# Moving work at the seams of a two-layer image kernel: moments of x, dummy matmuls, two normalisations and the last taps

## The reference

```python
# layer 0: linear attention, 6 heads of 64
x = x + attn(_gn(x))     # q, k = elu(rope(W x + b)) + 1 ; v = W x + b
                         # kv = sum_n k v ; out = q kv / (q . sum k + 1e-6) ; 1x1 conv Wfc
# layer 1: gated convolution
t = 1x1 conv(_gn(x))     # w_in
t = irfft2(rfft2(t, 8x8 patches) * fft_filter)
t = depthwise 3x3 conv(t); x1, x2 = halves of t
x = x + 1x1 conv(gelu(x1) * x2)   # w_out
# _gn: 32 groups of 12 channels, mean and variance over the group and all pixels
```

## Time and profile before

| | |
|---|---|
| median of 3 runs | 3602.86 us |
| the profiled execution's own time | 3610.5 us |
| its span, first to last instruction | 3608.4 us |
| PE busy | 3351.8 us (93%) |
| DVE busy | 3006.7 us (83%) |
| POOL busy | 2046.6 us (57%) |
| ACT busy | 1709.3 us (47%) |
| mean granted TensorE clock | 0.976 |

### The profile page before, as it was taken

The page is one execution under the profiler, slowest core; times in us unless marked ns, Lnnn a source line. Parts: engine busy times, 40 slices in busy tenths (PEclk is TensorE's granted clock), DMA queues, the critical chain, the costliest instruction groups (busy, mean ns, idle before and its releaser), DMA issues. The chain is left out here.

```text
span 3608.4 us, 50305 instructions
## 1 busy us (share of the span) xinstructions
PE 3351.8 (93%) x17430; PEld 2901.3 (80%) x17430; DVE 3006.7 (83%) x5252; ACT 1709.3 (47%) x3138; POOL 2046.6 (57%) x1343
## 2 busy tenths in 40 slices
PE   5999989999899999999999999999999999999998
PEld 4987779777797777977789777897778967799776
DVE  7977988779897698987989869788798887988877
ACT  1433844338443474434744357342574426644265
POOL 2554755547556474564755647456474565654555
PEclk9999999999999999999999999999999999999999
DMA  6214332143312333123321233312332133321422
GB/s 220 71 45 158 115 105 72 61 149 108 119 63 67 135 120 108 62 79 123 132 97 62 97 115 124 104 62 100 120 123 97 53 123 105 123 90 60 140 97 96
DMA packets 185339, 369.89 MB, mean 103 GB/s; under 512 B 7770, under 2 KB 8834, under 8 KB 184834
## 3 DMA queue, kind: packets, MB, share of 16 engines
q1 hardware_dynamic: 185090, 366.68, 29.7%
HBM read 265.99 MB, written 100.66 MB: 102 GB/s over the span
## 5 line engine op out<-in xcount | busy, mean ns | idle before, releaser
L1124 PE MATMUL bank<-w_hi,x_hi 128*128 128x384 f32 x2304 | 803.1, 349 | 19.3 <-ACT vt L575 10.0
L444 POOL TENSOR_TENSOR t<-t 128x768 f32<-128x768 f32 x256 | 534.8, 2089 | 468.8 <-DVE t L829 464.8
L1125 PE MATMUL bank<-w_lo,x_hi 128*128 128x384 f32 x2304 | 778.8, 338 | 0.0
L993 DVE SCALAR_TENSOR_TENSOR bank<-big,wdw,bank 128x512 f32<-128x512 f32 x1072 | 750.5, 747 | 22.4 <-PE bank L1305 19.4
L437 POOL TENSOR_TENSOR x_lo<-xa,x_hi 128x512 fp32r<-128x512 f32 x360 | 459.0, 1290 | 526.0 <-ACT x_hi L564 526.0
L509 POOL TENSOR_TENSOR prod<-prod 128x512 f32<-128x512 f32 x320 | 412.2, 1288 | 256.5 <-ACT prod L667 238.1
L1129 PE MATMUL bank<-w_hi,x_lo 128*128 128x384 f32 x2304 | 531.5, 339 | 0.5 <-POOL x_lo L437 0.5
L569 ACT ACTIVATE t<-t 128x384 f32<-128x384 f32 x256 | 134.7, 526 | 767.5 <-POOL t L444 749.9
L1124 PEld LDWEIGHTS bank<-w_hi,x_hi 128*128 128x128 f32 x2304 | 434.1, 188 | 26.4 <-issue 25.8
L1125 PEld LDWEIGHTS bank<-w_lo,x_hi 128*128 128x128 f32 x2304 | 434.9, 189 | 2.3 <-issue 1.7
L1129 PEld LDWEIGHTS bank<-w_hi,x_lo 128*128 128x128 f32 x2304 | 413.4, 188 | 1.4 <-POOL x_lo L437 1.4
(11 more groups left out here) (131 smaller groups left out, 7042.9 us busy)
## 6 DMA issues: line engine op xcount, KB each, us to landing
xr<-x SPq DMA_DIRECT2D x128, 768.0 KB, 4.8
xa<-x SPq DMA_DIRECT2D x64, 768.0 KB, 6.3
x_scratch<-xr SPq DMA_DIRECT2D x64, 768.0 KB, 3.3
xa<-x_scratch SPq DMA_DIRECT2D x64, 768.0 KB, 6.0
xr<-x_scratch SPq DMA_DIRECT2D x64, 768.0 KB, 4.9
out<-xr SPq DMA_DIRECT2D x64, 768.0 KB, 3.3
big<-x SPq DMA_DIRECT2D x8, 768.0 KB, 10.2
w_raw<-wqkv_t SPq DMA_DIRECT2D x1, 1728.0 KB, 7.0
```

Source lines behind the costliest of these rows:

```text
L444: nc.gpsimd.tensor_tensor(a, a, b[:, :, ::-1, :], ALU.add).then_inc(s_add, 1)
L993: nc.vector.scalar_tensor_tensor(dst, src, wdw[:, k, q:q + 1], so_far, ALU.mult, ALU.add)\
L1124: nc.tensor.matmul(dst, hi(k), whi(k), start=(k == 0), stop=False)
L1125: nc.tensor.matmul(dst, hi(k), wlo(k), start=False, stop=False)
```

## The change

Five edits, all of order or place. No arithmetic changes except that the next image's first chunk is normalised by ACT in the form x * rstd + shift instead of by DVE in the form (x - mean) * rstd.

1. The three `bn_aggr` of x leave `group_norm` and become `x_moments`, which DVE runs at the head of step 7 of stage B.
2. Dummies between the two averages: 2 instead of 6. After the second: 7 instead of 10.
3. In step 1 of stage C, ACT normalises and rounds chunk 2 right after its second `copy_t`, and POOL's `low_part` of it stands after two of the five additions.
4. In step 7 the next image's first chunk is normalised by ACT, at the place where steps 2 to 6 have their `normalise`.
5. In step 8 PE runs both sets of taps before the out blocks of chunk 6; in step 9 DVE runs all taps and both gates first, then the residuals of chunk 6, then `rope` of the next image. PE's wait ahead of `project` is split by block.

```diff
@@ part_c, gpsimd
+                    if c == 1:
+                        for k in range(KB):
+                            low_part(i * 16 + c + (NCH + 1), k, 1 - par, patches=(edge != NCH - 1))
...
-                    if within(edge, 0, NCH if i + 1 < images else NCH - 1):
+                    if c != 1 and c < (NCH if i + 1 < images else NCH - 1):
@@ part_c, scalar
                     if tile:
                         copy_t(T + 1, 1)
+                    if c == 1:
+                        normalise(1, i * 8 + 5 + h + par, 1 - par)
+                        high_part(i * 16 + c + (NCH + 1), 1 - par, patches=True)
...
-                        if within(edge, 0, NCH, 1) and edge != 0:
-                            normalise(i * 8 + 5 + h + par, 1 - par)
+                        if 1 < c < NCH - 1:
+                            normalise(1, i * 8 + 5 + h + par, 1 - par)
                         copy_img(T + 1, c, 1)
...
                         if edge == NCH - 1 and i + 1 < images:
+                            normalise(0, i * 8 + 9, 0)
                             high_part(i * 16 + 16, 0)
@@ vector
+            def x_moments(f):
+                dve.wait_ge(s_stat, f * NCH + NCH)
+                for k in range(KB):
+                    nc.vector.bn_aggr(mv[:, 0, k], bn_x[:, k].rearrange("p c s -> p (c s)"))
...
                 def part_b(c, h, edge, par):
+                    if c == NCH - 1:
+                        x_moments(i + 1)
...
                     if last:
-                        for m, early in enumerate((LAST[0:2], LAST[2:4], LAST[4:6])):
-                            for q, k in early:
-                                tap(c - 2, q, k, last)
-                            add_out(3, m)
+                        for q, k in LAST[:6]:
+                            tap(c - 2, q, k, last)
                         gate_narrow(c - 2, last)
-                        if i + 1 < images:
-                            rope((i + 1) * NT, 0, 0)
                         for q, k in LAST[6:]:
                             tap(c - 2, q, k, last)
                         gate_wide(c - 2, last)
+                        for m in range(KB):
+                            add_out(3, m)
+                        if i + 1 < images:
+                            rope((i + 1) * NT, 0, 0)
                         for m in range(KB):
                             add_out(2, m)
...
-                    if edge == NCH - 1 and i + 1 < images:
-                        normalise(0, i * 8 + 9, 0)
@@ tensor
                 keep_warm(14, 0)
-                group_avg(i + 1, 6, 0)
-                keep_warm(10, 0)
+                group_avg(i + 1, 2, 0)
+                keep_warm(7, 0)
...
                         taps(c - 1, 0, PE_LAST[0])
+                        taps(c - 1, 1, PE_LAST[1])
                         for b in range(KB):
                             out_block(c - 2, b)
-                        taps(c - 1, 1, PE_LAST[1])
                     if last:
-                        pe.wait_ge(s_res, (i * 16 + c + NCH - 2) * 3 + 6)
-                        if i + 1 < images:
-                            project((i + 1) * NT + 1, (i + 1) * 16, 0, 1, (0, 1))
+                        for b in range(2):
+                            pe.wait_ge(s_res, (i * 16 + c + NCH - 2) * 3 + (b + 5))
+                            if i + 1 < images:
+                                project((i + 1) * NT + 1, (i + 1) * 16, 0, 1, (b,))
```

More of the change, by code:

```diff
@@ L795, in group_norm @@
                 nxt(nc.vector.scalar_tensor_tensor(shift[:, :, :], gmean[:, :, :], -1.0, rstd[:, :, :], ALU.mult, ALU.mult), 11)
+            x_moments(0)
             group_norm(0)
```

14 lines of the change are left out of this document (6 added, 8 removed).

## The result

| | before | after |
|---|---|---|
| median, runs of one chip | 3603.9 us (4 runs, 3592.7 to 3609.8) | 3548.1 us (4 runs, 3545.7 to 3555.0) |
| the profiled execution's own time | 3610.5 us | 3545.7 us |
| its span | 3608.4 us | 3543.9 us |

The ratio is 0.9844, with a 95% interval of 0.9828 to 0.9859: 56 us faster. The forecast was 3530 with a range of 3508 to 3560.

What follows compares the result with a forecast made beforehand. PE, busy 93% of the span, was taken as the bound. Savings of 17.6 + 14.6 + 26.8 + 14.3 = 73.3 us, taken from the median of 3602.9, gave 3530 us, range 3508 to 3560 (own range 3515 to 3548).

Steps and rivals of the forecast that it cites:

- Seam: B-C seam: aggregations moved out and fewer dummies save 2.2 us per image, 17.6 over 8 images.
- Aggregations out: B-C seam: three aggregations leave the chain and hide in DVE's idle time, saving 0.76 us per image.
- Second averages behind dev: B-C seam: with 2 dummies instead of 6 they start 0.1 us after dev instead of 1.83; mean gain 1.45.
- Shift to dft: B-C seam: ACT's chain stays 5.95 us whatever PE does; three fewer dummies buy slack, not time.
- Rival 1: Seam and step 0: fewer dummies keep PE at 1.2 GHz, costing 24 us in all, 3554 us; chance 0.10.
- Steps 1 and 2: Stage C: moved normalise and low_part save 1.8 us per image, 14.6 over 8; steps take 14.7 and 19.5 us.
- Step 7: Stage C: normalising on ACT makes it a copy of step 6, saving 3.83 us an image, 26.8 over 7.
- Steps 8 and 9: Stage C's end: reordered taps, gates and residuals save 1.7 us per image, 11.7 over 7.
- From there PE is dense: Steps 8 and 9: from chunk 6's third out block PE runs without idle; 29.2 us stretch at full clock.
- The clock's share: Steps 8 and 9: clock expected to fall as often as before; 29.2 us at full clock, 30.8 below it.
- Rival 2: Step 7's wait moves to ACT, 3545 us, or the seam's bank wait takes 14 us, 3544 to 3560; chance 0.12.
- Last image: Last image, no projection: gate 3.4 us earlier, out blocks then wait for chunk 6; saves 2.6 us.

Runs made afterwards that it cites:

- e4: Changed kernel with the three aggregations of x moved back into the seam: 3554.0 us (one run).
- e3: Changed kernel with 6 and 10 dummies put back at the seam, as before the change: 3559.1 us, ratio to before 0.9872.
- e8: Changed kernel without the seven dummies behind the second averages: 3550.2 us, ratio to before 0.9842.
- e10: Changed kernel with chunk 6's residuals early around the last taps and step 7's normalise ahead of the second image copy: 3520.0 us, ratio to before 0.9763.
- e9: Changed kernel with normalise and low_part back in their old places in steps 1 and 7: 3578.3 us, ratio to before 0.9922.
- e5: Changed kernel with chunk 7's rounded gates given places of their own: 3528.8 us (one run).
- e7: Changed kernel with own places for chunk 7's rounded gates and 24 dummies ahead of chunk 6's third out block: 3532.1 us (one run).
- e12: Changed kernel with chunk 6's residuals early except in the last image, step 7's normalise ahead of the copy, own places for chunk 7's rounded gates: 3516.2 us.

## Why the prediction was right or wrong

- **Seam, right in kind, 5 us too small.** Aggregations out: 1.71 to 1.03 us from statistics to averages, 0.68 for 0.76. Second averages behind dev: 1.65 to 0.06, 1.59 for 1.45. Shift to dft 5.95: right. What the sum lacked is mostly 0.41 an image, 3.2 us in all, in the first averages (1.88 to 1.48 us from the first to the last start, mean): they ran at 2.4 GHz in all 8 images. PE's idle time ahead of them fell from 1.4 to 0.6 us in the mean. That this did it is well borne out: with the aggregations in the seam (before, e4) 8 of 16 first sets took over 1.6 us, in the twelve traces without them 6 of 96. Rival 1 did not come as a time, but its sign did. The Trainium skill ("TensorE: Matmul & The Clock Gate", section "The HAM clock gate") says that "the default state is throttled, and activity releases the throttle", so that fewer dummies mean a later release. The traces agree: from shift to the first dft the granted clock was 0.89 in e3 with its 16 dummies, 0.80 in the changed kernel and 0.58 in e8, and e3's second averages took 2.0 us against 2.5. The seam of e3 is 1.2 us an image longer all the same, since its dummies stand in the chain for 1.5.
- **Steps 1 and 2, right.** 14.71 and 19.40 us for 14.7 and 19.5; the last inverse waits for gb.
- **Step 7, right but for 0.27 us an image.** "Now ACT does them where it does them in steps 2 to 6" failed by one instruction: the normalise stands behind a copy that ACT has to wait for, 0.82 us, and PE gets 0.53 of it. Shown by e10.
- **Steps 8 and 9, wrong.** The forecast had PE idle until the third out block at 20.4 us behind the projection's start, which e9 hits (20.41). The step that failed is the next one: "From there PE is dense". It counted PE's matmuls and the banks, but not that chunk 7's rounding needs the places that this very block still reads. With the clock up it said 29.2; e9 shows 30.32, so the rounding takes 1.1 us of edit 5 (0.79 of it is PE's wait for g_lo in the row shown with e9), and the changed kernel shows 31.27, so the later sum of edit 4 takes another 0.95. That second loss is a cost of edit 4 that the prediction put at nothing ("DVE still starts at 1374.40"). The clock's share was allowed for at 1.1 us and was 0.8. 1.1 + 0.95 - 0.3 is about 1.8 us an image, as much as the whole gain of 1.7 that the forecast had there. Rival 2 named "the seam's new bank wait takes edit 5's gain" as the outcome, with 3544 to 3560, and that is where the time lies. The bank wait is real (3.51 us for the 2.7 that the forecast itself had), but alone it doesn't take the gain: the chain that it starts ends with the rounding, which no rival named.
- **Last image, wrong by 3.4 us** for the same reason: PE waits 4.12 us for g_lo there in the changed kernel. With places of their own and the same order (e5, e7, e12) the stretch is 3.5 to 5.9 us shorter.
- **The base.** By profiled executions the forecast was 3610.5 - 73.3 = 3537 and the measurement 3545.7. Half of the 18 us between 3530 and 3548 is due to the choice to take the saving from the median: the profiled execution of before lay 7 us above it. That part of what the sum counted (low clock in the seams) was special to that execution is argued, since there is one trace of before.
- **The total, right with luck.** Steps 8 and 9, the last image and step 7 fell short by 12.4, 3.4 and 1.9 us; the seams, steps 1 and 2 and all else gave 8.9 more than forecast and hid half of that. The range of 3508 to 3560 held the result, but it lies at the upper end of the forecast's own 3515 to 3548 and inside rival 2's.

Not settled: what of the all-else row (-3.2 us, stages A and B) is effect and what scatter; in the twelve other traces, with the same stages A and B, it moved between -3 and +5 us of the changed kernel's.

## What to carry to other kernels

When work is moved so that a wait becomes shorter, list for the instruction that comes next every resource it takes, buffers with a single place as well as banks, and ask who still reads them. A step that is made shorter on the critical engine does not make the side engines' work shorter: look at which of their results is needed right behind it, and what now runs beside it, since part of the gain is handed on. And "the same place as in the other steps" is to be read off the order of the engine's instructions, one by one: here a single copy in between cost 0.27 us in its step and 0.5 us in the next. And where an idle time can't be removed, put the instruction that ends it (here a residual of 0.7 us) as early as its inputs allow: that was worth more than the whole move of the taps.
